# A two-convolution residual block and a spline layer: residual added by DMA, polynomial by Horner, two waits and a table load moved

## The chip, the cores and the metric

The kernel runs on one core of one Trainium2 chip. A core has a matrix engine (PE, its weight loads are listed as PEld), a vector engine (DVE), an activation engine (ACT), GpSimd (POOL), a queue engine (SP) and 16 DMA engines; they run side by side and order themselves by semaphores. The metric is the device time of one execution in microseconds, the median over several runs.

## What is computed

x has the shape (32, 64, 56, 56) in fp32. The first part is a residual block:

```
out = relu(batchnorm(conv3x3(x, sign(w1))))
out = batchnorm(conv3x3(out, sign(w2)))
z   = relu(out + x)
```

The batch norms take mean and variance over the whole batch, so a convolution must be finished before its norm is known. The second part is a spline with clamped position, per element, with a curve for each of the 64 channels:

```
u = (clip(z*a + b, -1.5, 1.5) + 1) * 0.5 * 31;  i = floor(u);  t = clip(u - i, 0, 1)
y = id_gain*z + bias + sum_r mix[c,r] * (alpha[i-1,r]*b0(t) + alpha[i,r]*b1(t) + alpha[i+1,r]*b2(t) + alpha[i+2,r]*b3(t))
```

b0 to b3 are the cubic basis polynomials; the four knot indices are clipped to 0..31.

## The kernel before

Two images lie on the 128 partitions (2 x 64 channels), which makes 16 pairs. The convolutions go through the pairs, each image split in a high and a low fp16 part, and write y1 and y2 to scratch in DRAM. `norm` computes a scale and a bias (BN2_S, BN2_B) on DVE after each of them, with one square root on ACT (line 427).

The spline works on chunks: half a pair, 128 x 1568 elements, 32 chunks in all, two or three in flight. A position is brought to a fixed-point number; its high part is a cell, its low part a signed distance (`offset`) from the nearest of 17 centres. For each chunk and channel five piecewise constant tables are needed: T_NEAR (cube), T_FAR (the cube beyond a distance of 1), T_SQ, T_LIN and T_VAL. PE sums each table in PSUM as steps times 0/1 masks: T_NEAR and T_FAR take four groups of masks ("quads"), the other three take two. PSUM holds two tables at a time, so PE may start a table only when DVE has used the one two places before it (`table`, wait on `table_used`); the order is NEAR, FAR, SQ, LIN, VAL, then NEAR of the next chunk.

What one chunk asks of the others, by the names of the code:

- SP: `load` brings the chunk of y2 to `zbuf` (called `place`) and the chunk of x to `lin` (line 871; it waits until the output that used this `lin` before is stored), `spread` copies the cells to four partition groups in 16 DMAs, `store` writes `lin` out.
- DVE: `total` (line 1016, lin = zbuf * BN2_S + x), `fixed` (1022), `linear` (1028), `near_cube` (1067), `far_cube` (1075), `far_part` (1083), two `middle` masks (1045), `add_table` for T_SQ (1090), `near_part` (1098, times the squared distance), `slope` (1105, T_LIN times offset), `add_slope` (1113), `offsets` (1037), `add_table` for T_VAL (1090) and `finish` (1121, lin = poly * AMP + lin).
- ACT: `far_distance` (961), `position` (930, from `lin` to `zbuf`), `far_square` (968), `cells` (938), `distance_square` (975), `distance` (954), and two `edge` masks (982).
- POOL: `add_far` (919), a DMA that adds the `far` tile onto `lin`, once a chunk.

The work of one loop body belongs to several chunks: in the body of chunk c, DVE finishes c-1 and sums the masks of c+1, and `total`, `position`, `fixed`, `linear`, `cells`, `spread` and `offsets` belong to c+2. The order is the order of the code; each engine has its own. ACT's engine and DVE's wait in place, so what stands behind a waiting instruction waits too.

Between the two parts stands the end of a block: all engines meet there, and SP comes to it only after its waits for the y2 stores.

## Time and profile before

| | us |
|---|---|
| median of 3 runs | 1256.26 (1254.87 to 1257.54) |
| profiled execution, whole | 1254.66 |
| its span, first to last instruction | 1252.8 |
| DVE busy | 1062.8 (85%) |
| PE busy | 1058.6 (85%) |
| ACT busy | 868.8 (69%) |
| POOL busy | 113.4 (9%) |

The busy shares are means over stages that differ: the convolutions fill roughly the first 427 us, the spline the rest. In the spline a busy share near one on an engine says that work in its own order is never late there; a wait printed behind a row ("<-") names what came last before the row could start. A figure "x56" is a count of instructions. An idle wait of an engine that is not the last one costs nothing, so the rows have to be read in pairs: who waits, and what the releaser itself was doing before.

### The profile page before, as it was taken

What the parts mean: (1) busy time and instruction counts of PE and PEld (TensorE: products, weight loads), DVE (VectorE), ACT (ScalarE), POOL (GpSimd) and SP (SyncE); (2) the same over time, 40 slices, a digit from 0 to 9 for tenths busy, and PEclk for the clock granted to TensorE, in tenths of its full rate; (3) what the DMA queues carried; (4) which work ended last, traced back from release to release, by engine and by line L of the source; (5) the groups of instructions that cost most, each with busy time, mean ns of one, the idle gap of its engine ahead of it and who ended that gap; (6) DMA issues with size and microseconds to landing.
All of it is one profiled execution on the core that took longest, in us unless ns stands there. A gap on an engine that the chain in (4) does not pass through costs nothing. (4 is left out here: it accounts for less than half of the span.)

```text
span 1252.8 us, 51454 instructions
## 1 busy us (share of the span) xinstructions
PE 1058.6 (85%) x23562; PEld 710.2 (57%) x23562; DVE 1062.8 (85%) x951; ACT 868.8 (69%) x424; POOL 113.4 (9%) x189
## 2 busy tenths in 40 slices
PE   6999996999999368887888788878887888788876
PEld 4688885788888234554545455444544545455444
DVE  5765656766666689999999999999999999999987
ACT  4454544777787267688868877887788778877881
POOL 6000000282000000000000000000000000000000
PEclk9999998999999778998989889898998989889898
DMA  7666766576777386677767766777677667776552
GB/s 227 259 257 256 276 255 225 217 277 252 271 264 300 136 235 181 183 216 194 185 189 213 196 181 193 208 192 184 189 214 192 184 197 206 194 182 197 157 114 78
DMA packets 58215, 260.85 MB, mean 208 GB/s; under 512 B 16336, under 2 KB 16336, under 8 KB 50000
## 3 DMA queue, kind: packets, MB, share of 16 engines
q1 hardware_dynamic: 52528, 230.88, 56.3%
q0 software_dynamic: 4608, 25.69, 11.0%
q8 instruction: 139, 2.28, 0.8%
q10 hardware_dynamic: 928, 1.90, 0.6%
q14 instruction: 12, 0.10, 0.0%
HBM read 104.29 MB, written 77.07 MB: 145 GB/s over the span
## 5 line engine op out<-in xcount | busy, mean ns | idle before, releaser
L1181 PE MATMUL tab<-edge_mask,diag 128*32 128x392 bf16 x10240 | 501.8, 358 | 132.6 <-DVE poly L1090 130.8
L1181 PEld LDWEIGHTS tab<-edge_mask,diag 128*32 128x32 f16 x10240 | 281.7, 104 | 339.0 <-DVE poly L1090 143.4
L982 ACT ACTIVATE edge_mask<-cell,thr 128x6272 bf16<-128x6272 bf16 x62 | 338.5, 5508 | 0.0
L711 PE MATMUL acc<-split,w 64*64 64x392 f16 x4608 | 195.9, 329 | 12.0 <-DVE w L463 10.8
L711 PE MATMUL acc<-band_split,w 64*64 64x392 f16 x4608 | 197.9, 330 | 9.4 <-ACT band_split L368 7.2
L410 ACT ACTIVATE yout<-acc 128x1568 f32<-128x1568 f32 x64 | 94.2, 1473 | 160.6 <-PE acc L711 139.4
L1181 PE MATMUL tab<-middle_mask,diag 128*32 128x392 bf16 x4096 | 183.4, 332 | 25.0 <-DVE middle_mask L1052 25.0
L711 PEld LDWEIGHTS acc<-band_split,w 64*64 64x64 f16 x4608 | 164.1, 107 | 42.9 <-issue 14.1
L711 PEld LDWEIGHTS acc<-split,w 64*64 64x64 f16 x4608 | 155.3, 107 | 51.9 <-issue 12.6
L520 DVE BATCH_NORM_STATS2 stats<-yout 128x392 f32 (+1 forms) x240 | 118.0, 555 | 60.2 <-ACT yout L410 59.4
L930 ACT ACTIVATE zbuf<-lin,cst 128x1568 f32<-128x1568 f32 x32 | 54.3, 1697 | 163.8 <-DVE lin L1016 157.9
L1181 PEld LDWEIGHTS tab<-middle_mask,diag 128*32 128x32 f16 x4096 | 107.7, 99 | 92.2 <-DVE middle_mask L1052 25.1
L919 POOL DMA_DIRECT2D lin<-far x32 | 50.0, 1564 | 897.5 <-DVE far L1083 897.5
L1090 DVE SCALAR_TENSOR_TENSOR poly<-tab,first,poly 128x1568 f32<-128x1568 f32 x61 | 112.6, 1845 | 0.1
L1045 DVE TENSOR_SCALAR middle_mask<-cell,thr 128x6272 bf16<-128x6272 bf16 x62 | 111.9, 1847 | 0.0
L486 DVE SCALAR_TENSOR_TENSOR band_split<-band_split,xin 128x1568 f16<-128x1568 f16 x30 | 52.5, 1793 | 35.0 <-ACT band_split L389 35.0
L1075 DVE SCALAR_TENSOR_TENSOR far<-tab,first,far 128x1568 f32<-128x1568 f32 x31 | 57.3, 1847 | 8.8 <-PE tab L1181 8.6
L497 DVE SCALAR_TENSOR_TENSOR split<-split,xin 128x3136 f16<-128x3136 f16 (+4 forms) x19 | 55.1, 2913 | 10.7 <-ACT split L400 10.5
L1083 DVE SCALAR_TENSOR_TENSOR far<-far,cst,far_sq 128x1568 f32<-128x1568 f32 x32 | 59.3, 1852 | 2.9
L1016 DVE SCALAR_TENSOR_TENSOR lin<-zbuf,cst,lin 128x1568 f32<-128x1568 f32 x32 | 59.0, 1846 | 3.1 <-PEq L90 3.1
L1121 DVE SCALAR_TENSOR_TENSOR lin<-poly,cst,lin 128x1568 f32<-128x1568 f32 x31 | 57.4, 1852 | 3.3
L1113 DVE SCALAR_TENSOR_TENSOR poly<-far_sq,poly 128x1568 f32<-128x1568 f32 x32 | 57.4, 1793 | 3.1
(126 smaller groups left out, 816.9 us busy)
## 6 DMA issues: line engine op xcount, KB each, us to landing
y_scratch<-yout SPq DMA_DIRECT2D x32, 1568.0 KB, 6.2
cell<-cell SPq DMA_DIRECT2D x496, 98.0 KB, 3.3
xin<-y_scratch SPq DMA_DIRECT2D x16, 1568.0 KB, 9.0
zbuf<-y_scratch SPq DMA_DIRECT2D x32, 784.0 KB, 5.9
lin<-in_x SPq DMA_DIRECT2D x32, 784.0 KB, 6.1
lin<-far POOLq DMA_DIRECT2D x32, 784.0 KB, 8.8
out<-lin SPq DMA_DIRECT2D x31, 784.0 KB, 4.1
xin<-in_x SPq DMA_DIRECT2D x15, 1568.0 KB, 9.3
```

What stands on the lines that cost most here:

```text
L410: act.activation(yout[b][:, :].rearrange("p (r k x) -> p k r x", r=2, k=TILES)[:, 2 * part:2 * part + 2], acc[:, 4 * part:4 * part + 4, 0: ...
L520: dve.bn_stats(stats[:, bass.ds(COUNTS * (g - base) + t, 1), :], yout[b][:, own]).then_inc(counted, 1)
L711: mm = pe.matmul(acc[h * C:(h + 1) * C, 2 * k + r, 0:TILE], weights[part][own, tap * C:(tap + 1) * C], image[own, first:first + ROWS, dx:d ...
L982: act.activation(mask_of(b, q)[:, :, :], cell4[b % 2][:, :, :], ACT.Sign, bias=thr[:, q:q + 1]).then_inc(sign_mask_ready, 1)
L1016: dve.scalar_tensor_tensor(out=lin[b % BUFS][:, :], in0=place[b % 2][:, :], scalar=cc(BN2_S), in1=lin[b % BUFS][:, :], op0=ALU.mult, op1=A ...
L1045: dve.tensor_scalar(mask_of(b, q)[:, :, :], cell4[b % 2][:, :, :], thr[:, q:q + 1], None, ALU.is_ge).then_inc(mask_ready, 1)
L1075: dve.scalar_tensor_tensor(out=quarters(far), in0=summed(i, b, T_FAR), scalar=base(i, b, T_FAR), in1=quarters(far), op0=ALU.add, op1=ALU.m ...
L1083: dve.scalar_tensor_tensor(out=far[:, :], in0=far[:, :], scalar=cc(AMP), in1=far_sq[:, :], op0=ALU.mult, op1=ALU.mult).then_inc(far_part_r ...
L1090: dve.scalar_tensor_tensor(out=quarters(poly[b % 2]), in0=summed(i, b, t), scalar=base(i, b, t), in1=quarters(poly[b % 2]), op0=ALU.add, o ...
L1113: dve.scalar_tensor_tensor(out=poly[b % 2][:, :], in0=far_sq[:, :], scalar=1 / POINT, in1=poly[b % 2][:, :], op0=ALU.mult, op1=ALU.add).th ...
L1121: dve.scalar_tensor_tensor(out=lin[b % BUFS][:, :], in0=poly[b % 2][:, :], scalar=cc(AMP), in1=lin[b % BUFS][:, :], op0=ALU.mult, op1=ALU. ...
L1181: mm = pe.matmul(tab[(b + t) % 2][j * GROUP:(j + 1) * GROUP, sub, 0:SUB], keep["diag"][part][:, j % 2, t, q, :], mask_of(b, q)[:, j, sub * ...
```

## The change

1. x is no longer loaded by SP and added by DVE. ACT writes y * BN2_S into `lin` (`scale`), and POOL issues a DMA that adds the chunk of x from DRAM onto it (`add_x`); `position` then waits for that DMA. It is done for chunks 2 to 31; chunks 0 and 1 keep `total`. ACT scales chunk c+3 in the body of chunk c, and POOL issues `add_x(c+3)` behind `add_far(c)`.
2. The polynomial is evaluated as ((near + sq)*d + lin)*d + val with the signed distance d: `near_part`, `slope` and `add_slope` become `times_offset`, `add_table` and `times_offset`. The squared distance (`distance_square` on ACT) is gone, and with it a tile.
3. On DVE `fixed` stands ahead of `near_cube`, where `total` stood.
4. SP's waits for the last y2 stores move from the end of the convolution block to behind the first spread of the spline block, and `load` stands ahead of `store`.
5. The first ACTIVATE of the kernel is a square root in place of an identity.
6. Two mask tiles change places in memory, and semaphores count by one.

```diff
-        stored = [sem(f"y_stored{b}") for b in range(2)]
+        stored = keep["y_stored"]
...
@@ -283,8 +283,6 @@
             for b in range(2):
                 sp.wait_ge(stored[b], 16 * half_rounds)
             rounds(sp, 1, lambda i, n: body(i, n, y2, 1))
-            for b in range(2):
-                sp.wait_ge(stored[b], 32 * half_rounds)
...
-            act.activation(tmp[:, 5:6], row_scale[:, 0:1], ACT.Identity)
+            act.activation(tmp[:, 5:6], row_scale[:, 0:1], ACT.Sqrt)
...
+        middle_mask = [sb(f"middle_mask{q}", [P, 4, CHUNK], BF16) for q in range(len(MIDDLE_QUADS))]
         edge_mask = [[sb(f"edge_mask{s}{q}", [P, 4, CHUNK], BF16) for q in range(len(EDGE_QUADS))] for s in range(2)]
-        middle_mask = [sb(f"middle_mask{q}", [P, 4, CHUNK], BF16) for q in range(len(MIDDLE_QUADS))]
...
-        dist_sq = sb("dist_sq", [P, CHUNK])
...
@@ -862,13 +860,10 @@
             def load(i, b):
 
                 ysrc = part(y2, i, b)
-                xsrc = part(x, i, b)
-                before, free = in_front(sp, BUFS * i + b - 1), in_front(sp, 16 * (i + b // BUFS))
+                before = in_front(sp, BUFS * i + b - 1)
                 wait_past(sp, offset_ready, before)
                 wait_past(sp, cell_ready, before)
                 sp.dma_start(place[b % 2][:, :], ysrc).then_inc(y_loaded[b % 2], 16)
-                wait_past(sp, stored[b % BUFS], free)
-                sp.dma_start(lin[b % BUFS][:, :], xsrc).then_inc(x_loaded[b % BUFS], 16)
...
             spread(0, 0)
+            for b in range(2):
+                sp.wait_ge(keep["y_stored"][b], 16 * PAIRS)
             load(0, 2)
             spread(0, 1)
 
             def body(i, b, n):
+                if exists(n, b + 3):
+                    load(i, b + 3)
                 if exists(n, b - 1):
                     store(i, b - 1)
-                if exists(n, b + 3):
-                    load(i, b + 3)
                 if exists(n, b + 2):
                     spread(i, b + 2)
...
+            def add_x(c):
+
+                pool.wait_ge(scaled, c - 1)
+                pool.dma_start(lin[c % BUFS][:, :], x[c // 2][:, (c % 2) * CHUNK:(c % 2 + 1) * CHUNK],
+                               accum_op=ALU.add).then_inc(x_added, 16)
+
             def add_far(c):
 
-                pool.wait_ge(far_part_ready, 2 * c + 2)
+                pool.wait_ge(far_part_ready, c + 1)
                 pool.dma_start(lin[c % BUFS][:, :], far[:, :], accum_op=ALU.add).then_inc(far_added, 16)
 
+            add_x(2)
             for c in range(CHUNKS):
                 add_far(c)
+                if c + 3 < CHUNKS:
+                    add_x(c + 3)
...
+            def scale(i, b):
+
+                c = BUFS * i + b
+                act.wait_ge(y_loaded[b % 2], 16 * (2 * i + b // 2 + 1))
+                wait_past(act, stored[b % BUFS], 16 * (i + b // BUFS))
+                act.activation(lin[b % BUFS][:, :], place[b % 2][:, :], ACT.Identity,
+                               scale=cc(BN2_S)).then_inc(scaled, 1)
+
             def position(i, b):
 
                 c = BUFS * i + b
-                act.wait_ge(sum_ready, c + 1)
+                if isinstance(c, int) and c < 2:
+                    act.wait_ge(sum_ready, c + 1)
+                else:
+                    act.wait_ge(x_added, 16 * (c - 1))
                 act.activation(place[b % 2][:, :], lin[b % BUFS][:, :], ACT.Identity, bias=cc(U_B),
                                scale=cc(U_S)).then_inc(place_ready, 1)
...
                 act.wait_ge(far_ready, c + 1)
-                wait_past(act, slope_ready, 2 * c)
+                wait_past(act, far_part_ready, c)
                 act.activation(far_sq[:, :], far[:, :], ACT.Square).then_inc(far_sq_ready, 1)
-
-            def distance_square(i, b):
-
-                c = BUFS * i + b
-                act.wait_ge(offset_ready, c + 1)
-                wait_past(act, near_ready, 2 * c)
-                act.activation(dist_sq[:, :], offset[b % 2][:, :], ACT.Square,
-                               scale=1 / POINT).then_inc(dist_sq_ready, 1)
...
             distance(0, 0)
+            scale(0, 2)
 
             def body(i, b, n):
-                following, after = exists(n, b + 1), exists(n, b + 2)
+                following, after, third = exists(n, b + 1), exists(n, b + 2), exists(n, b + 3)
                 far_distance(i, b)
                 if after:
                     position(i, b + 2)
                 far_square(i, b)
                 if after:
                     cells(i, b + 2)
-                distance_square(i, b)
                 if following:
                     distance(i, b + 1)
-                    edge(i, b + 1, EDGE_QUADS[0])
+                if third:
+                    scale(i, b + 3)
                 if following:
-                    edge(i, b + 1, EDGE_QUADS[1])
+                    for q in EDGE_QUADS:
+                        edge(i, b + 1, q)
 
             rounds(act, body)
...
                 dve.wait_ge(fixed_ready, c + 1)
-                wait_past(dve, dist_sq_ready, c - 1)
-                wait_past(dve, slope_ready, 2 * (c - 2) + 1 if not isinstance(c, int) or c >= 2 else 0)
+                wait_past(dve, slope_ready, c - 1 if not isinstance(c, int) or c >= 2 else 0)
...
-            def near_part(i, b):
-
-                c = BUFS * i + b
-                dve.wait_ge(table_used, used(i, b, T_SQ))
-                dve.wait_ge(dist_sq_ready, c + 1)
-                dve.tensor_tensor(poly[b % 2][:, :], poly[b % 2][:, :], dist_sq[:, :], ALU.mult).then_inc(near_ready, 2)
-
-            def slope(i, b):
-
-                c = BUFS * i + b
-                dve.wait_ge(far_part_ready, 2 * c + 2)
-                dve.wait_ge(table_ready, used(i, b, T_LIN))
-                dve.scalar_tensor_tensor(out=quarters(far_sq), in0=summed(i, b, T_LIN), scalar=base(i, b, T_LIN),
-                                         in1=quarters(offset[b % 2]), op0=ALU.add, op1=ALU.mult).then_inc(table_used, 1)
-
-            def add_slope(i, b):
-
-                c = BUFS * i + b
-                dve.wait_ge(table_used, used(i, b, T_LIN))
-                dve.wait_ge(near_ready, 2 * c + 2)
-                dve.scalar_tensor_tensor(out=poly[b % 2][:, :], in0=far_sq[:, :], scalar=1 / POINT,
-                                         in1=poly[b % 2][:, :], op0=ALU.mult, op1=ALU.add).then_inc(slope_ready, 2)
+            def times_offset(i, b, t, done):
+
+                dve.wait_ge(table_used, used(i, b, t))
+                dve.scalar_tensor_tensor(out=poly[b % 2][:, :], in0=offset[b % 2][:, :], scalar=1 / POINT,
+                                         in1=poly[b % 2][:, :], op0=ALU.mult, op1=ALU.mult).then_inc(done, 1)
...
             def body(i, b, n):
                 previous, following, after = exists(n, b - 1), exists(n, b + 1), exists(n, b + 2)
                 if previous:
-                    add_table(i, b - 1, T_VAL, slope_ready, 2 * (BUFS * i + b - 1) + 2)
+                    add_table(i, b - 1, T_VAL, slope_ready, BUFS * i + b)
                     finish(i, b - 1)
                 if after:
-                    total(i, b + 2)
+                    fixed(i, b + 2)
                 near_cube(i, b)
                 if after:
-                    fixed(i, b + 2)
                     linear(i, b + 2)
                 far_cube(i, b)
                 far_part(i, b)
@@ -1163,9 +1155,9 @@
                     for q in MIDDLE_QUADS:
                         middle(i, b + 1, q)
                 add_table(i, b, T_SQ, table_used, used(i, b, T_NEAR))
-                near_part(i, b)
-                slope(i, b)
-                add_slope(i, b)
+                times_offset(i, b, T_SQ, near_ready)
+                add_table(i, b, T_LIN, near_ready, BUFS * i + b + 1)
+                times_offset(i, b, T_LIN, slope_ready)
                 if after:
                     offsets(i, b + 2)
 
```

DVE, in the opening of the spline, from the last table of chunk 0 to the far cube of chunk 1 (`zbuf` is the position, `lin` the sum, `tab` the table in PSUM), before:

```order
L1090 SCALAR_TENSOR_TENSOR poly<-tab,plain,poly 128x1568
L1121 SCALAR_TENSOR_TENSOR lin<-poly,cst,lin 128x1568
L1016 SCALAR_TENSOR_TENSOR lin<-zbuf,cst,lin 128x1568
L1067 SCALAR_TENSOR_TENSOR poly<-tab,first,poly 128x1568
L1022 TENSOR_SCALAR zbuf<-zbuf,cst 128x1568
L1028 TENSOR_SCALAR lin<-lin,cst,par_sb 128x1568
L1075 SCALAR_TENSOR_TENSOR far<-tab,first,far 128x1568
```

and the same place now:

```order
L1100 SCALAR_TENSOR_TENSOR poly<-tab,plain,poly 128x1568
L1114 SCALAR_TENSOR_TENSOR lin<-poly,cst,lin 128x1568
L1033 TENSOR_SCALAR zbuf<-zbuf,cst 128x1568
L1077 SCALAR_TENSOR_TENSOR poly<-tab,first,poly 128x1568
L1039 TENSOR_SCALAR lin<-lin,cst,par_sb 128x1568
L1085 SCALAR_TENSOR_TENSOR far<-tab,first,far 128x1568
```

The sum is gone, and the clamp to fixed point (`fixed`) has moved ahead of the near cube. The other DVE instructions of a chunk keep their number and place.

ACT, at the start of the spline, from the distance of chunk 0 to the masks of chunk 1 (`edge_mask`), before:

```order
L954 ACTIVATE poly<-offset 128x1568
L961 ACTIVATE far<-poly,cst 128x1568
L930 ACTIVATE zbuf<-lin,cst 128x1568
L968 ACTIVATE far_sq<-far 128x1568
L938 ACTIVATE cell<-zbuf,cst 128x1568
L975 ACTIVATE dist_sq<-offset 128x1568
L954 ACTIVATE poly<-offset 128x1568
L982 ACTIVATE edge_mask<-cell,thr 128x6272 x2
```

and now:

```order
L971 ACTIVATE poly<-offset 128x1568
L937 ACTIVATE lin<-zbuf,cst 128x1568
L978 ACTIVATE far<-poly,cst 128x1568
L947 ACTIVATE zbuf<-lin,cst 128x1568
L985 ACTIVATE far_sq<-far 128x1568
L955 ACTIVATE cell<-zbuf,cst 128x1568
L971 ACTIVATE poly<-offset 128x1568
L937 ACTIVATE lin<-zbuf,cst 128x1568
L991 ACTIVATE edge_mask<-cell,thr 128x6272 x2
```

Line 937 is `scale`; it stands once ahead of the far distance of chunk 0 and then once a body between the distance and the masks. The squared distance is gone.

POOL's queue was 32 times `add_far`. It now begins:

```order
L916 DMA lin<-in_x 128x1568
L922 DMA lin<-far 128x1568
L916 DMA lin<-in_x 128x1568
L922 DMA lin<-far 128x1568
L916 DMA lin<-in_x 128x1568
L922 DMA lin<-far 128x1568
```

Line 916 is `add_x`, of chunks 2, 3 and 4 here; line 922 is `add_far`, of chunks 0, 1 and 2.

## Rows read from the trace of the kernel before

**Rows 1.** Windows, the spline stage: busy time and count of each engine, granted clock, DMA

```profile
427.00:1253.00 826.00, 663.28 (x14336) 389.41 (x14336) 789.02 (x488) 621.23 (x254) 50.04 (x32) 0.90 0.69 185
```

**Rows 2.** Waits, 484 to 1200 us: total us, times, longest

```profile
PE tab L1181 <- DVE poly L1090: 122.5, 29, 4.4
...
DVE far L1075 <- PE tab L1181: 1.9, 7, 0.4
```

**Rows 3.** Timeline of DVE, one chunk: start us, us, instruction

```profile
859.48 1.84 DVE L1075 SCALAR_TENSOR_TENSOR far<-tab,first,far 128x1568 f32<-128x1568 f32 x1
861.42 1.85 DVE L1083 SCALAR_TENSOR_TENSOR far<-far,cst,far_sq 128x1568 f32<-128x1568 f32 x1
...
866.71 1.84 DVE L1090 SCALAR_TENSOR_TENSOR poly<-tab,first,poly 128x1568 f32<-128x1568 f32 x1
...
872.30 1.79 DVE L1113 SCALAR_TENSOR_TENSOR poly<-far_sq,poly 128x1568 f32<-128x1568 f32 x1
...
878.76 1.84 DVE L1016 SCALAR_TENSOR_TENSOR lin<-zbuf,cst,lin 128x1568 f32<-128x1568 f32 x1
880.52 1.84 DVE L1067 SCALAR_TENSOR_TENSOR poly<-tab,first,poly 128x1568 f32<-128x1568 f32 x1
...
884.73 1.85 DVE L1075 SCALAR_TENSOR_TENSOR far<-tab,first,far 128x1568 f32<-128x1568 f32 x1 [0.26 <-PE tab L1181]
```

**Rows 4.** Timeline of PE, two chunks, and windows over one's first table

```profile
618.58 4.19 PE L1181 MATMUL tab<-edge_mask,diag 128*32 128x392 bf16 x64 [4.39 <-DVE poly L1090]
...
868.61 5.42 PE L1181 MATMUL tab<-edge_mask,diag 128*32 128x392 bf16 x64 [4.39 <-DVE poly L1090]
...
881.85 8.13 PE L1181 MATMUL tab<-edge_mask,diag 128*32 128x392 bf16 x192
...
868.60:873.80 5.20, 5.19 (x64) 2.52 (x68) 5.06 (x3) 5.20 (x1) 0.00 (x0) 0.50 0.85 176
```

**Rows 5.** Timelines of DVE and PE, the last two chunks, which have no total

```profile
1216.74 1.85 DVE L1090 SCALAR_TENSOR_TENSOR poly<-tab,first,poly 128x1568 f32<-128x1568 f32 x1
...
1233.89 1.85 DVE L1075 SCALAR_TENSOR_TENSOR far<-tab,first,far 128x1568 f32<-128x1568 f32 x1 [3.46 <-PE tab L1181]
...
1218.64 4.52 PE L1181 MATMUL tab<-edge_mask,diag 128*32 128x392 bf16 x64 [3.95 <-DVE poly L1090]
```

**Rows 6.** Groups of ACT, 484 to 1185 us: busy us, mean ns, idle before

```profile
L930 ACT ACTIVATE zbuf<-lin,cst 128x1568 f32<-128x1568 f32 x28 | 47.5, 1698 | 144.2 <-DVE lin L1016 144.2
...
L975 ACT ACTIVATE dist_sq<-offset 128x1568 f32<-128x1568 int32 x28 | 41.9, 1497 | 0.0
```

**Rows 7.** DMA: line 919 (add_far), queue q0 500 to 1200, load of x

```profile
DMA to landing us min/median/max: 5.9/8.8/12.1
...
q0 software_dynamic: 4032, 22.48, 17.3%
...
lin<-in_x SPq DMA_DIRECT2D x32, 784.0 KB, 6.1
```

**Rows 8.** Timelines at the ends of both convolutions, and the last y2 store

```profile
211.31 1.28 ACT L427 ACT_TABLE_LOAD   x1
...
212.89 0.16 DVE L650 RECIPROCAL tmp<-tmp 128x1 f32<-128x1 f32 x1 [0.98 <-ACT tmp L427]
...
421.36 0.35 SPq L274 DMA_DIRECT2D y_scratch<-yout  x1
...
422.22 0.16 DVE L650 RECIPROCAL tmp<-tmp 128x1 f32<-128x1 f32 x1 [0.25 <-ACT tmp L427]
...
427.49 1.85 DVE L1016 SCALAR_TENSOR_TENSOR lin<-zbuf,cst,lin 128x1568 f32<-128x1568 f32 x1 [3.08 <-PEq L90]
...
y_scratch<-yout SPq DMA_DIRECT2D x1, 1568.0 KB, 5.1
```

**Rows 9.** Timeline of ACT and DVE at the spline's start

```profile
452.90 1.60 ACT L961 ACTIVATE far<-poly,cst 128x1568 f32<-128x1568 f32 x1
...
459.44 1.85 DVE L1075 SCALAR_TENSOR_TENSOR far<-tab,plain,far 128x1568 f32<-128x1568 f32 x1 [1.04 <-PE tab L1181]
```

More of the change, by code:

```diff
@@ L798, in spline @@
         stored = [sem(f"out_stored{b}") for b in range(BUFS)]
+        x_added = sem("x_added")
         far_added = sem("far_part_added")
+        scaled = sem("scaled")
         sum_ready = sem("sum_ready")
@@ L808, in spline @@
         far_sq_ready = sem("far_sq_ready")
-        dist_sq_ready = sem("dist_sq_ready")
         mask_ready = sem("mask_ready")
@@ L1083, in far_part @@
                 dve.scalar_tensor_tensor(out=far[:, :], in0=far[:, :], scalar=cc(AMP), in1=far_sq[:, :],
-                                         op0=ALU.mult, op1=ALU.mult).then_inc(far_part_ready, 2)
+                                         op0=ALU.mult, op1=ALU.mult).then_inc(far_part_ready, 1)
             def add_table(i, b, t, made, count):
@@ L1126, in closing_quarters @@
                 last, b = CHUNKS // BUFS - 1, BUFS - 1
-                dve.wait_ge(slope_ready, 2 * CHUNKS)
+                dve.wait_ge(slope_ready, CHUNKS)
                 dve.wait_ge(far_added, 16 * CHUNKS)
@@ L1243, in build @@
             "lin": [sb(f"lin{b}", [P, CHUNK]) for b in range(BUFS)],
+            "y_stored": [sem(f"y_stored{b}") for b in range(2)],
             "y_loaded": [sem(f"y_loaded{b}") for b in range(2)],
```

## Prediction, written before the changed kernel ran

> **What bounds the kernel now.** I first read the windows by stage. In the spline DVE is busy 789 of 826 us, ACT 621 and PE 663, at a mean granted clock of 0.90 [rows 1]. That makes DVE look like the only bound, and an instruction taken from it like pure gain. The waits say less: DVE waits for PE only 1.9 us in all, before `far_cube`, but PE waits for DVE 29 times, 122.5 us [rows 2], or 4.2 us a chunk, always before the same table, T_VAL, whose place in PSUM `add_table` of T_SQ frees. So I read one chunk in order, from that release.
>
> On DVE the release ends at 866.71 + 1.84 = 868.55 (call it s), and the next `far_cube` starts at 884.73, s + 16.2; from that start to the next release are 866.71 - 859.48 + 1.84 = 9.07 us [rows 3]. A chunk is the sum, 25.25 us there, and 24.98 on average: the `far_cube` of chunk 0 starts at 459.44 and that of chunk 31 at 1233.89, 31 intervals [rows 5, 9]. DVE waited 0.26 us in this chunk, so of the 16.2 us it fills 15.9 itself.
>
> On PE, s releases T_VAL, then come T_NEAR and T_FAR of the next chunk without a gap. T_VAL took 5.42 us here and 4.19 in another chunk; the window over it shows a granted clock of 0.50, the lower level of 1.2 GHz, after an idle time of 4.39 us [rows 4]. The clock is back at 2.4 GHz for the rest: 192 matmuls take 8.13 us, 2.66 for 64 (starts overlap the listed ends by 0.15), so the 256 matmuls of NEAR and FAR take 10.6. FAR is complete at s + 0.06 + 5.2 + 10.6 + 0.2 = s + 16.1, which is where `far_cube` started. With the T_VAL of 4.19 (4.0 start to start) it is s + 14.9. So the two engines are within 1 us of each other over this stretch, and only the other 9.07 us are DVE's alone.
>
> The last chunks are the experiment that the kernel itself makes: no `total`, `fixed`, `linear` or `offsets` stand between. The release ends at 1216.74 + 1.85 = 1218.59, `far_cube` starts at 1233.89, s + 15.3, after 3.46 us of waiting for PE, whose T_VAL took 4.52 at the low clock [rows 5]. Some 4.7 us of DVE work taken away (`total` 1.76, `fixed` and `linear` 3.95 - 1.85 = 2.1 [rows 3], `offsets` about 0.9) moved `far_cube` from about s + 15.9 by 0.6. That is the row on which my forecast rests.
>
> **The change, part by part.** The sum is made against the profiled execution, 1254.66 us whole; the median of the runs is 1256.26, 1.6 above it, and I add that at the end.
>
> Square root first: the first batch norm waits 0.98 us for ACT, behind a table load of 1.28, the second 0.25 with no load [rows 8]. The load goes, and the identities, relus and signs run after a square root in both programs: -0.7. The Trainium skill, ScalarE: Activation LUTs, What ACT_TABLE_LOAD costs, puts a switch at 2.66 us with its drain; by it the term would be up to -2.7, but the trace's load is hidden in part, and the 1.28 row agrees with the page's 1283 ns for the load proper.
>
> The y2 wait: the last store is issued at 421.36 and takes 5.1 us, so it lands at 426.5; DVE had been idle 3.08 us when it began at 427.49, 1.0 after the landing [rows 8]. Without the wait the blocks meet when DVE is done, at 424.4, and the same 1.0 follows: -2.1. Behind the moved wait on SP stands the load of chunk 2, which is not issued until the first spread is out, long after; nothing pays for it. Bounds: 0 to -3.
>
> Spline's start: this is new waiting. Before, the far distance of chunk 0 starts on ACT at 452.9 and the first `far_cube` at 459.44 [rows 9]. Now `scale` of chunk 2 (not shown by this trace; 1.5 to 1.7 by the two ACT passes [rows 6]) comes ahead, then POOL issues `add_x`, which must land before `position`, and DVE's `fixed` stands ahead of its first near cube. Chain, in the old times: 452.9 + 1.6 + 0.3 to the issue, landing 5.9 at least and 8.8 at the median of the only such DMA [rows 7], `position` 1.7, then `fixed`, near cube and `linear`, 884.73 - 0.26 - 880.52 = 3.95 [rows 3]: `far_cube` at 466.4 to 469.3 in place of 459.44. The DMA is nearly alone there, so I take a landing of 6.5 and a loss of +7.5 (bounds +7 to +10; a load of x by SP takes 6.1).
>
> Each chunk, DVE: `total` goes, 1.76 start to start [rows 3]; three polynomial passes stay three, all fp32 at 1.79 to 1.85; but each now waits for the one before it, one more such dependence of about 0.15. `fixed` only changes place. DVE could be at `far_cube` at s + 15.9 - 1.6 = s + 14.3, and its own period would be 23.4.
>
> Each chunk, PE: NEAR still cannot start before `add_table` of T_LIN has ended, s + 3.9. If the clock does not fall, FAR is there at s + 3.9 + 10.6 + 0.2 = s + 14.7, a period of 23.8. If it falls as now, s + 14.9 to 16.1 [rows 4], s + 15.3 in [rows 5]: periods of 24.0 to 25.2. What PE idles before T_VAL shrinks only from 4.2 to about 3.7, because that idle time lies in the 9.07 us that stay (9.07 less SQ and LIN, 5.3); at 3.95 the clock still fell [rows 5]. So it falls in most chunks, with a slow stretch that has a little less idle time in it. I take 24.3 on average, near the last chunks' 15.3 + 9.07 = 24.4. That is 0.7 less than 24.98; it counts in the 29 intervals in which a `total` stood: -19.7 (bounds 23.8 and 25.0: -34 to 0).
>
> Each chunk, DMA: `far_part` ends, POOL issues `add_far` 0.3 later and `add_x(c+3)` 1.6 behind it on the same queue. From 500 to 1200 us the 28 `add_far` took 17.3% of the 16 engines' 700 us, 4.3 us each [rows 7], so x needs about 4 to 5.5 us behind the landing of `add_far` at 8.8: 12.8 to 14.3 after the first issue (call it X). Behind X stand `position` 1.75, 3.95 for `fixed`, near cube and `linear`, then `far_cube` to the end of `far_part`, 861.42 + 1.85 - 859.48 = 3.8: the loop closes in X + 9.8. Up to X = 14.5 it fits in 24.3. I charge +3 for the few landings near the 12.1 maximum, which would each stretch a chunk by about 2. ACT exchanges a pass of 1.5 for one of 1.6; it waits 144.2 us in 28 chunks [rows 6], 5.1 each, which covers that and the wait for the stored output that `scale` inherits from SP's load. SP loses a DMA a chunk, and the y2 load no longer stands behind a store. Nothing for these, with up to +3 if the cover fails in places. The Trainium skill, DMA: Bandwidth & Descriptors, Anatomy of one DMA, fits such a DMA as 2.0 us plus bytes over 436 GB/s, an estimate of 3.8 us for 803 KB. No row agrees with it here, the shortest accumulation is 5.9 and the median 8.8; by the page X would be under 9 and the queue no subject at all.
>
> Sum: 1254.66 - 0.7 - 2.1 + 7.5 - 19.7 + 3 = 1242.7, and with the 1.6 to the median 1244.3. I predict 1244.
>
> **The rivals.**
>
> A. The DVE count is all that matters: 1.6 a chunk. For it speaks DVE's share in [rows 1]; against it the 3.46 us of waiting as soon as work goes [rows 5]. 1256.3 - 2.8 + 7.5 - 29 x 1.6 = 1215.
>
> B. The clock holds because PE idles less: period 23.8, -34. 1256.3 - 2.8 + 7.5 - 34 = 1227. Against it speaks that it fell after 3.95.
>
> C. Slower: POOL's queue becomes the loop. It decides from X = 15.2, where X + 9.8 is the old 24.98. Were the two accumulations to land one full latency after the other, X would be 17.6, the period 27.4 and the time 1256 + 29 x 2.4 + 5 = 1331; an X of 16 gives 25.8 and 1285. For it: one DMA already reached 12.1, x comes from DRAM and not from the core's own memory, and masks are being spread at the same moment. Against: the data of `add_far` keep the engines busy only about 4 of its 8.8 us, so the second one's fixed part lies beside the first.
>
> D. PE gives nothing back: the low clock covers T_VAL wholly in every chunk (s + 16.1), or the queue takes the 0.7 (X about 15). Then only start and block end are left, 1256.3 - 2.8 + 7.5 = 1261 at the worst, 1254 to 1261 in all.
>
> **How the numbers follow.** Forecast (periods of 24.0 to 24.6, 1234 to 1253): 0.66. A: 0.04. B: 0.10. C: 0.10. D: 0.10. The range is 1228 to 1260: it leaves out A, half of B's low side and nearly all of C. A change within 0.2%, 2.5 us, cannot be told from none here. Faster takes the forecast, A, B, which is 0.80; same, 1253.7 to 1258.8, most of D, 0.08; slower C and the rest of D, 0.12.
>
> **What would show it.** After: `far_cube` waiting for PE about 1 us in most chunks, T_VAL still in 4 to 5.4 us behind an idle time of about 3.7, and the starts of `far_cube` 24.3 apart. DVE's first `far_cube` near 464.5. No table load at 211, no 3 us of idle time before the spline's first DVE instruction. Landings of the x accumulation 11 to 13 us after their issue, and ACT's `position` waiting for them little. If `position` waits for `add_x` in every chunk and `fixed` waits for `position`, C holds. If the far cube does not wait for PE at all, A. If the clock shows full in the T_VAL windows, B. The weakest number is X, because no row has two accumulations back to back.

## The result, and the profile after

The changed kernel takes 1269.05 us, the median of 4 runs (1268.45 to 1271.71); the kernel before took 1256.38 in the same comparison. The ratio is 1.0108 [1.0093, 1.0123]: 1.1% slower, where 1244 us had been forecast, outside the range of 1228 to 1260. Two of the twelve executions of kernel 1 below fell in a slow state (1440.2 and 2160.7 us); they are in its median of 1256.04 and not in its ratio.

The forecast had named what to look at. The starts of the kernel came out as forecast. Timelines of DVE in the changed kernel (start us, us, instruction, in brackets the idle time ahead and what ended it), at the first batch norm, at the spline's first instruction and at its first far cube:

```profile
211.93 0.16 DVE L648 RECIPROCAL tmp<-tmp 128x1 f32<-128x1 f32 x1 [0.26 <-ACT tmp L425]
...
425.54 1.85 DVE L1027 SCALAR_TENSOR_TENSOR lin<-zbuf,cst,lin 128x1568 f32<-128x1568 f32 x1 [0.98 <-PEq L90]
...
461.42 1.09 DVE L1033 TENSOR_SCALAR zbuf<-zbuf,cst 128x1568 int32<-128x1568 f32 x1 [11.74 <-ACT zbuf L947]
...
465.20 1.84 DVE L1085 SCALAR_TENSOR_TENSOR far<-tab,plain,far 128x1568 f32<-128x1568 f32 x1
```

The wait of 0.98 behind the table load is 0.26, the 3.08 ahead of the spline is 0.98 [rows 8], and the first far cube starts at 465.20 (464.5 had been forecast; the terms of the sum, 459.44 + 7.5 - 2.8, give 464.1; 459.44 before [rows 9]). What came after it did not. The waits of the steady stretch, 500 to 1200 us (total us, times, longest):

```profile
ACT zbuf L947 <- DMA lin<-in_x: 125.1, 28, 6.1
...
PE tab L1173 <- DVE poly L1100: 109.4, 27, 4.3
...
DVE zbuf L1033 <- ACT zbuf L947: 55.3, 28, 3.3
...
DVE far L1085 <- PE tab L1173: 3.5, 6, 0.9
```

The first and third rows are the mark that the forecast had set for its rival C: in every chunk `position` waits for `add_x` and `fixed` waits for `position`. DVE's far cube hardly waits for PE. The source view of the two accumulations gives their landings (line 916, `add_x`, then line 922, `add_far`):

```profile
DMA to landing us min/median/max: 8.2/14.1/15.4
...
DMA to landing us min/median/max: 5.8/9.4/10.5
```

`add_x` is issued 1.6 us behind `add_far`, so X is 1.6 + 14.1 = 15.7 where 12.8 to 14.3 had been assumed. The chain of waits, followed back through one chunk (start us, us, what the time belongs to), shows that nothing else is in the loop:

```profile
864.94 1.70 ACT zbuf L947
...
866.67 0.05 DVE zbuf L1033
...
867.68 0.43 DVE poly L1077
...
869.45 0.55 DVE lin L1039
...
870.45 1.86 DVE far L1085
...
872.33 1.86 DVE far L1093
...
874.48 1.58 POOL lin L922
876.05 13.99 DMA lin<-in_x
```

From the issue at 874.48 the landing at 890.04 is 15.6 away; before the issue lie 9.54 us, from the start of `position` on. The whole is 25.1, and the far cubes of chunks 1 to 29 are 25.35 apart on average (25.03 before). The loop has no slack, so each late landing is paid in full. Of the whole kernel's chain the page gives to this one DMA:

```profile
DMA lin<-in_x 21%; PE tab L1173 17%; DVE far L1085 4%; DVE middle_mask L1055 4%; DVE far L1093 3%; ACT zbuf L947 3%; POOL lin L922 2%; DVE poly L1100 2%; DVE poly L1077 1%; DVE lin L1039 1%; ACTq L963 1%; DVE poly L1106 0%; ACT cell L955 0%; DVE zbuf L1033 0%; DVE lin L1129 0%
```

DVE is busy 1012.6 us now and was busy 1062.8 before: 50 us of work left the engine with the largest share, and the kernel became slower.

### The profile page after: what moved, and what is told of

It is laid out like the page before. It is cut to its first block, busy times and chain, and to the rows that moved or that the text cites. A ratio compares the mean times of both kernels' runs of the same rounds, so it can differ in the third digit from the quotient of the medians.

```text
span 1267.8 us, 51281 instructions
## 1 busy us (share of the span) xinstructions
PE 1068.0 (84%) x23562; PEld 726.9 (57%) x23562; DVE 1012.6 (80%) x921; ACT 871.0 (69%) x421; POOL 165.0 (13%) x219
## 4 chain that ended last, share of the span: by engine, by line
DMA 21%; PE 17%; DVE 16%; issue 6%; ACT 3%; POOL 2%; ACTq 1%; DVEq 0%
DMA lin<-in_x 21%; PE tab L1173 17%; DVE far L1085 4%; DVE middle_mask L1055 4%; DVE far L1093 3%; ACT zbuf L947 3%; POOL lin L922 2%; DVE poly L1100 2%; DVE poly L1077 1%; DVE lin L1039 1%; ACTq L963 1%; DVE poly L1106 0%; ACT cell L955 0%; DVE zbuf L1033 0%; DVE lin L1129 0%
## 5 line engine op out<-in xcount | busy, mean ns | idle before, releaser
L1173 PE MATMUL tab<-edge_mask,diag 128*32 128x392 bf16 x10240 | 508.3, 358 | 141.6 <-DVE poly L1100 124.2
L1173 PEld LDWEIGHTS tab<-edge_mask,diag 128*32 128x32 f16 x10240 | 292.1, 104 | 343.4 <-DVE poly L1100 136.8
L709 PEld LDWEIGHTS acc<-band_split,w 64*64 64x64 f16 x4608 | 167.6, 107 | 39.7 <-issue 13.1
L1100 DVE SCALAR_TENSOR_TENSOR poly<-tab,first,poly 128x1568 f32<-128x1568 f32 x92 | 169.9, 1847 | 3.3
L1173 PEld LDWEIGHTS tab<-middle_mask,diag 128*32 128x32 f16 x4096 | 110.4, 99 | 90.3 <-DVE middle_mask L1062 22.9
L1106 DVE SCALAR_TENSOR_TENSOR poly<-offset,poly 128x1568 f32<-128x1568 int32 x64 | 114.7, 1792 | 2.2
L1033 DVE TENSOR_SCALAR zbuf<-zbuf,cst 128x1568 int32<-128x1568 f32 x32 | 35.1, 1096 | 76.5 <-ACT zbuf L947 76.5
L916 POOL DMA_DIRECT2D lin<-in_x x30 | 52.4, 1747 | 159.9 <-ACT lin L937 159.9
L978 ACT ACTIVATE far<-poly,cst 128x1568 f32<-128x1568 f32 x32 | 51.3, 1602 | 27.1 <-DMA lin<-far 27.1
## 6 DMA issues: line engine op xcount, KB each, us to landing
lin<-in_x POOLq DMA_DIRECT2D x30, 784.0 KB, 14.1
```

The costliest lines, as they stand in the source:

```text
L709: mm = pe.matmul(acc[h * C:(h + 1) * C, 2 * k + r, 0:TILE], weights[part][own, tap * C:(tap + 1) * C], image[own, first:first + ROWS, dx:d ...
L1100: dve.scalar_tensor_tensor(out=quarters(poly[b % 2]), in0=summed(i, b, t), scalar=base(i, b, t), in1=quarters(poly[b % 2]), op0=ALU.add, o ...
L1106: dve.scalar_tensor_tensor(out=poly[b % 2][:, :], in0=offset[b % 2][:, :], scalar=1 / POINT, in1=poly[b % 2][:, :], op0=ALU.mult, op1=ALU. ...
L1173: mm = pe.matmul(tab[(b + t) % 2][j * GROUP:(j + 1) * GROUP, sub, 0:SUB], keep["diag"][part][:, j % 2, t, q, :], mask_of(b, q)[:, j, sub * ...
```

## The experiments

Each kernel is timed against the kernel before, on the same chip. "Period" is the mean distance of the far cubes of chunks 1 to 29; "first" is where the first far cube starts. Both are read from the one profiled execution, while "us" is the median of all.

| kernel | us | ratio to before | first | period |
|---|---|---|---|---|
| before | 1256.4 | 1 | 459.4 | 25.03 |
| after | 1269.05 | 1.0108 [1.0093, 1.0123] | 465.2 | 25.35 |
| 1 fixed behind near cube | 1256.04 | 1.0009 [0.9994, 1.0024] | 461.1 | 24.96 |
| 2 x ahead of far | 1233.51 | 0.9826 [0.9809, 0.9843] | 465.1 | 24.31 |
| 3 no far accumulation | 1228.67 | 0.9781 [0.9766, 0.9796] | 465.2 | 24.01 |
| 4 before, waits and square root | 1252.40 | 0.9974 [0.9964, 0.9984] | 457.4 | 25.03 |
| 5 both 1 and 2 | 1247.89 | 0.9944 [0.9929, 0.9959] | 461.4 | 24.61 |
| 6 all but the x part | 1252.23 | 0.9973 [0.9964, 0.9983] | 456.0 | 25.03 |
| 7 x part adds a tile | 1243.05 | 0.9897 [0.9880, 0.9914] | 463.5 | 24.51 |
| 8 half of x | 1237.80 | 0.9863 [0.9848, 0.9877] | 462.7 | 24.29 |
| 9 2, and a shorter start | 1226.47 | 0.9769 [0.9756, 0.9782] | 457.6 | 24.26 |
| 10 SP and tiles as before | 1261.68 | 1.0049 [1.0031, 1.0067] | 466.3 | 25.11 |
| 11 before, x part alone | 1267.96 | 1.0092 [1.0076, 1.0107] | 470.5 | 25.13 |
| 12 9, with store ahead of load | 1266.20 | 1.0080 [1.0061, 1.0100] | 457.2 | 25.64 |

**1. Take the near cube out of the loop.**

```diff
-                if after:
-                    fixed(i, b + 2)
                 near_cube(i, b)
                 if after:
+                    fixed(i, b + 2)
                     linear(i, b + 2)
```

> The changed kernel with one edit: fixed stands behind near_cube on DVE again. Theory L (a loop through POOL's queue sets the period: far_part, add_far, add_x behind it, position, fixed, near_cube, linear, far_cube, far_part, X + 9.8 with X = 1.6 + 14.1 = 15.7, 25.5 us a chunk): near_cube, 1.8 us, leaves the loop, which then closes in 23.7, so the far table on PE is last again at about 24.3; 29 x 1.0 less and 1.8 less at the start, about 1239 us. Rival R (16 DMA engines are too full and everything behind them is late alike, or the Horner passes cost it): the wait only moves to another instruction, 1267 to 1270.

It gave back 13 us, the whole loss, but not the 30 that were expected. The waits from 500 to 1200 us:

```profile
ACT zbuf L947 <- DMA lin<-in_x: 113.6, 27, 6.1
...
DVE far L1085 <- PE tab L1172: 30.8, 23, 2.9
PE tab L1172 <- issue: 16.3, 16, 2.1
```

`position` is as late as ever for x, and now PE's share appears: the far cube waits for it 30.8 us, and PE itself loses 16.3 us in 16 places that the profile calls issue. The cells, and ACT's edge masks of the next chunk, stand behind `position` on ACT, and in the timeline all 16 stops fall in tables made of edge masks. That the late masks cause them is a reading and was not tried by itself. Without the near cube the loop should close in X + 8.0 = 23.6, so what sets the 24.96 of this kernel is not shown; 16.3 us of stops in 28 chunks, 0.6 each, would lift PE's 24.3 to about that. What is shown is that taking the near cube from behind the wait gives back the whole loss, 4.1 us of it before the first far cube, although `position` waits for x almost as before.

**2. Issue the x accumulation first.**

```diff
             for c in range(CHUNKS):
-                add_far(c)
                 if c + 3 < CHUNKS:
                     add_x(c + 3)
+                add_far(c)
```

> The changed kernel with one edit: POOL issues add_x(c+3) ahead of add_far(c). Theory L: x is issued when ACT has scaled, about 1.7 us before far_part ends, and no longer waits behind 4 us of far's data; position then waits for far_distance, that is for add_far, which now lands 12 to 13 us after its issue. The loop closes in 0.3 + 12.5 + 1.6 + 1.75 + 3.95 + 3.8 = 23.9, so about 24.3 a chunk and 1242 to 1248 us. Rival R (the amount of accumulation, not its order): the same bytes, the same period, 1267 to 1270.

Swapping two lines moved the kernel from 1269 to 1233.5, better than expected. The source views, `add_x` and then `add_far`:

```profile
DMA to landing us min/median/max: 7.4/8.2/9.1
...
DMA to landing us min/median/max: 5.9/11.2/13.5
```

The 14.1 of x is 8.2, and `add_far` has taken over the queueing, 11.2 for 9.4. `far_distance` waits for that landing, and `position` stands right behind `far_distance` on ACT. So from the issue of `add_far` to the start of `position` the loop now takes 11.2 and 1.5 for `far_distance`, where X was 15.7: about 3 us less. The bytes are the same as in the changed kernel, so the amount of accumulation alone does not make the loss. In the timelines of POOL, ACT, DVE and PE, and in the window over T_VAL, the new order is seen at work:

```profile
869.87 1.68 ACT L947 ACTIVATE zbuf<-lin,cst 128x1568 f32<-128x1568 f32 x1
...
877.14 1.85 DVE L1085 SCALAR_TENSOR_TENSOR far<-tab,first,far 128x1568 f32<-128x1568 f32 x1 [0.65 <-PE tab L1173]
...
878.67 0.86 POOL L916 DMA_DIRECT2D lin<-in_x  x1 [19.80 <-ACT lin L937]
881.18 1.59 POOL L922 DMA_DIRECT2D lin<-far  x1 [1.65 <-DVE far L1093]
...
886.22 4.14 PE L1173 MATMUL tab<-edge_mask,diag 128*32 128x392 bf16 x64 [3.83 <-DVE poly L1100]
...
886.22:890.20 3.98, 3.98 (x65) 2.17 (x68) 3.82 (x3) 2.98 (x1) 0.00 (x0) 0.66 1.00 221
```

`scale` releases `add_x` 2.5 us ahead of `add_far` (at the median x is issued 1.9 us after the start of the far cube, where it was 5.6 in the changed kernel); `position` has no wait of its own; and the far cube waits 0.65 us for PE (28.6 us in 26 chunks of 500 to 1200 us), whose T_VAL still takes 4.14 us, at a mean granted clock of 0.66, behind an idle time of 3.83. That is the picture that had been forecast for the changed kernel (about 1 us of waiting, 3.7 idle). The period, 24.31, is the forecast's too, but this profiled execution took 1238.8 us and was the slowest of five; the 5.3 us down to the median put the period there nearer 24.1.

**3. Leave the other accumulation out.** `add_far` isn't issued, so the far part is missing from the result, and its waiters wait for `far_part`.

```diff
             for c in range(CHUNKS):
-                add_far(c)
                 if c + 3 < CHUNKS:
                     add_x(c + 3)
```

> The changed kernel without the DMA add_far: the far part is computed and never added, and what waited for its landing waits for far_part. Theory L: add_x is alone in its queue, lands 8 to 9 us after its issue, well before position; the period is the one that the prediction put on PE and DVE, 24.3 (23.8 to 24.6), so 1236 to 1244 us. Rival D (PE gives nothing back, the low clock covers the gain): 24.8 or more, 1255 or more. Rival A (DVE alone): 23.4, about 1215.

The period fell to 24.01. The x accumulation lands in 9.1 us at the median:

```profile
DMA to landing us min/median/max: 7.3/9.1/10.2
```

Against 2 the rest of POOL's queue is worth 0.3 us a chunk by the profiled executions, 0.2 by the medians. The far cube waits for PE in all 29 chunks of the stretch, 27.6 us, so PE is last at a period of 24.0. Its clock is low in T_VAL here too: the one at 883.55 takes 4.14 us at a mean of 0.66. The forecast of B (23.8 with a full clock) is nearly the same number for another reason.

**4 and 6. The parts without x.** In 4 the kernel before gets the square root and the moved wait; in 6 the changed kernel gets back `total`, SP's load of x and the order of `store` and `load`, and so keeps Horner, the wait and the square root.

```diff
-                sp.wait_ge(stored[b], 32 * half_rounds)
+                sp.wait_ge(keep["y_stored"][b], 16 * PAIRS)
...
-            act.activation(tmp[:, 5:6], row_scale[:, 0:1], ACT.Identity)
+            act.activation(tmp[:, 5:6], row_scale[:, 0:1], ACT.Sqrt)
```

> The kernel before with two parts of the change only: the first ACTIVATE is a square root, and SP's waits for the y2 stores stand behind the first spread of the spline. All theories: 0.7 + 2.1 less, 1253.5 us; no table load at 211 us, DVE's first spline instruction about 1 us after its last one of the block before.

```diff
                 if after:
-                    fixed(i, b + 2)
+                    total(i, b + 2)
                 near_cube(i, b)
                 if after:
+                    fixed(i, b + 2)
                     linear(i, b + 2)
```

> The change without its first part: x is loaded by SP and summed by DVE as before, the Horner form, the moved y2 wait and the early square root stay. Theory L: the Horner passes wait each for the one before, 0.15 a chunk more on DVE, which is the bound here again: 1252.4 + 4, 1255 to 1257 us. Rival H (the Horner form is what made the change slow): 1262 or more.

Both come to 1252.3: 3.3 us gained by the ratio, for the two waits (2.8 had been forecast), and nothing from Horner, neither way; the 4 us that had been expected in 6 for its longer chain of waits did not come. Their period is the 25.03 of before.

**5. Both orders at once.** The edits of 1 and 2 together.

```diff
+                near_cube(i, b)
                 if after:
                     fixed(i, b + 2)
-                near_cube(i, b)
-                if after:
                     linear(i, b + 2)
```

> The changed kernel with both edits: add_x ahead of add_far on POOL, and fixed behind near_cube on DVE. Theory L: with x first the loop through POOL is already shorter than what PE and DVE need (24.3 a chunk), so taking near_cube out of it gives nothing more per chunk; the first near cube no longer waits for x, 1.9 less at the start: 1230 to 1235 us against the 1233.5 of x first alone. Rival S (fixed is what ACT's cells wait for, and the masks behind them are late on PE): slower than x first alone, 1238 or more.

Wrong by 13 us: it is slower than 2 alone. The waits of 500 to 1200 us:

```profile
ACT far L978 <- DMA lin<-far: 100.3, 29, 4.5
...
DVE lin L1114 <- DMA lin<-far: 27.3, 23, 2.5
ACT lin L937 <- DMA out<-lin: 26.0, 15, 3.1
```

and the timeline of POOL and of DVE around one pair of issues:

```profile
858.54 1.60 POOL L916 DMA_DIRECT2D lin<-in_x  x1 [20.18 <-ACT lin L937]
860.13 1.77 POOL L922 DMA_DIRECT2D lin<-far  x1
...
873.53 1.85 DVE L1114 SCALAR_TENSOR_TENSOR lin<-poly,cst,lin 128x1568 f32<-128x1568 f32 x1 [1.52 <-DMA lin<-far]
```

`near_cube` ahead of `fixed` brings the cells, and with them `scale`, about 2 us later with respect to the far cube. `scale` now ends when `far_part` does (858.24 and 858.25), the head start of x is gone, and `add_far` is issued behind it, 1.9 us after the end of `far_part` where 0.3 would do. DVE's `finish` waits for it. That the queue is the loop again, entered at its other end, is one reading. The other is the rival that stood in the expectation, late masks: PE has 9 stops called issue here, 6.4 us, all in tables made of edge masks, and none in 2. Over the whole stretch `finish` waits for `add_far` 27.3 us (1.6 in 2), and `scale` waits for the stored output 26.0 us (11.7 in 2), so the cells are not all that delays it. The run does not tell these shares apart; the period is 0.3 us longer than in 2, 8 us in 28 chunks.

**7 and 8. What makes x late.** In 7 `add_x` adds a tile of zeros from the core's memory, of the same size, so the residual is left out for these chunks; in 8 it adds only half of the columns of x.

```diff
-                pool.dma_start(lin[c % BUFS][:, :], x[c // 2][:, (c % 2) * CHUNK:(c % 2 + 1) * CHUNK],
+                pool.dma_start(lin[c % BUFS][:, :], still[:, :],
```

> The changed kernel with one edit: add_x reads a tile of zeros in the core's own memory in place of x in DRAM, so the residual is left out. Theory L with the source as its cause: the second accumulation lands about 4 us behind the first, X = 14.3 in place of 15.7, a period of 24.3 and 1242 to 1250 us. If the place in the queue alone decides: it lands 6 us behind as before, and the time stays at 1265 to 1270.

```diff
-                pool.dma_start(lin[c % BUFS][:, :], x[c // 2][:, (c % 2) * CHUNK:(c % 2 + 1) * CHUNK],
+                pool.dma_start(lin[c % BUFS][:, 0:CHUNK // 2], x[c // 2][:, (c % 2) * CHUNK:(c % 2) * CHUNK + CHUNK // 2],
```

> The changed kernel with one edit: add_x moves only the first 784 of the 1568 columns, so half of the residual is left out. Theory L: half of x's data leaves the queue, about 2.3 us; X = 13.4, the loop closes in 23.2 and the far table on PE is last, 24.0 to 24.4 a chunk, 1236 to 1243 us. Rival F (a fixed latency per DMA, not its data, is what position waits for): landing at 13 us or more, 1260 or more.

Landings of `add_x` in 7 and in 8:

```profile
DMA to landing us min/median/max: 7.2/12.4/14.1
...
DMA to landing us min/median/max: 5.7/11.1/13.2
```

X is 14.0 with a tile as the source, 12.7 with half the bytes, 15.7 in the changed kernel. Both dropped under the point where the loop decides, and both kernels fell near PE's floor. A source in DRAM is 1.7 us of the 15.7, and the second half of the bytes 3.0. Most of the 1.7 is not in x's own part: `add_far` itself lands after 8.1 in 7, where it took 9.4.

**10 and 11. The rest of the change put back, and x alone.** 10 is the changed kernel with SP's `store` ahead of `load` and the mask tiles in their old places; 11 is the kernel before with the x part only.

```diff
-                if exists(n, b + 3):
-                    load(i, b + 3)
                 if exists(n, b - 1):
                     store(i, b - 1)
+                if exists(n, b + 3):
+                    load(i, b + 3)
```

> The changed kernel with SP's order (store ahead of load) and the place of the two mask tiles as before. Both theories put no time on these: 1267 to 1270 us, X within 0.3 us of 15.7. If they matter, the time moves by more than 3 us.

> The kernel before with the first part of the change alone (x accumulated by DMA, total gone from chunk 2 on, fixed ahead of near_cube); the old polynomial, the old waits and the table load stay. Theory L: the loop through POOL's queue does not contain the polynomial behind far_part, so the period is 25.4 as in the whole change, and the start costs the same: 1269 + 2.8 = 1270 to 1274 us. If the Horner form had a share in the slowing, this one is faster than the whole change.

The x part alone costs 11.6 us by the ratio, so it is the main cause; the whole change costs 13.6 by the same measure. 10 came 7 us under the changed kernel where at most 3 were expected. So the x part costs 11.6, the two waits give 3.3, and `load` ahead of `store` or the places of the mask tiles cost another 7; that these add up to 15 and not 13.6 is within the intervals. Its waits and the landing of `add_x`:

```profile
ACT zbuf L947 <- DMA lin<-in_x: 99.6, 27, 6.1
...
ACT lin L937 <- DMA zbuf<-y_scratch: 41.3, 24, 5.5
...
DMA to landing us min/median/max: 8.1/13.7/15.1
```

The load of y2 is issued 3.4 us later with respect to the far cube, after x has landed, and `scale` has to wait for it; in this order of POOL's queue that costs nothing, since `add_x` stands behind `add_far`. The landing of x is 0.4 shorter at the median. Taken one by one over chunks 1 to 28, X is 15.64 on average in the changed kernel, 15.37 in 10 and 15.29 in 11, which also has the old order and places, with a period of 25.13. 28 times the 0.27 is 7.6 us, so a shorter X accounts for the size. Why X is shorter stays open: that the earlier load of y2 in the changed kernel slows x by sharing the engines would fit, but the two edits of 10 were not tried apart.

**9 and 12. The best version, and a warning.** 9 is 2, and besides chunk 2 is summed by `total` as chunks 0 and 1 are, with its `fixed` behind the near cube of chunk 0, so that the opening is as before. 12 is 9 with SP's `store` ahead of `load`.

```diff
+                if isinstance(i, int) and i == 0 and b == 2:
+                    sp.dma_start(lin[b][:, :], part(x, i, b)).then_inc(x_loaded[b], 16)
...
+                opening = isinstance(i, int) and i == 0 and b == 0
+                if opening:
+                    total(i, b + 2)
```

> The changed kernel with add_x ahead of add_far, and with chunk 2 handled as chunks 0 and 1: SP loads its x, DVE sums it in the body of chunk 0, fixed(2) stands behind near_cube(0) there. Theory L: the steady part is that of x first alone (24.3 a chunk), and the spline's start loses its 11.7 us wait for position: the first far cube at 457.5 in place of 465.1, so 1225 to 1229 us against 1233.5. Rival: the first chunks have slack elsewhere and the 7.5 us come back in the next bodies, 1231 or more.

> The kernel of e9_start with SP's store ahead of its load again. The output's store then does not share the engines with the load of y2, so scale waits less for it (11.7 us over 27 chunks with x first) and x is issued a little earlier: 0 to 3 us less than e9_start. If far's landing or the far table on PE is last anyway: the same.

9 took 7 us from 2, as expected: the first far cube is at 457.6 in place of 465.1. It beats the kernel before by 2.3% and the changed one by 3.4%. 12, for which 0 to 3 us less were expected, is 40 us slower than 9. Timelines of SP, ACT, POOL and DVE in 12, one chunk:

```profile
861.20 1.85 DVE L1114 SCALAR_TENSOR_TENSOR lin<-poly,cst,lin 128x1568 f32<-128x1568 f32 x1 [3.25 <-DMA lin<-far]
...
863.08 0.35 SPq L888 DMA_DIRECT2D out<-lin  x1
863.74 1.22 SPq L866 DMA_DIRECT2D zbuf<-y_scratch  x1
...
870.86 1.60 ACT L938 ACTIVATE lin<-zbuf,cst 128x1568 f32<-128x1568 f32 x1 [2.17 <-DMA zbuf<-y_scratch]
...
872.75 1.06 POOL L918 DMA_DIRECT2D lin<-in_x  x1 [23.12 <-ACT lin L938]
873.81 1.77 POOL L924 DMA_DIRECT2D lin<-far  x1
...
887.16 1.85 DVE L1114 SCALAR_TENSOR_TENSOR lin<-poly,cst,lin 128x1568 f32<-128x1568 f32 x1 [1.46 <-DMA lin<-far]
```

This is a closed ring: `finish` (861.20) releases `store`, the load of y2 stands behind it (863.74) and is there at 870.8, `scale`, `add_x`, and behind that `add_far` (873.81), whose landing releases the next `finish` at 887.16, 25.96 later. In this chunk every member waits for the one before it; from 500 to 1200 us `scale` waits for the load of y2 27 times and `finish` for `add_far` 21 times. Harmless in 10, the order of `store` and `load` on SP closes the ring as soon as x stands first on POOL's queue.

## Why the prediction was wrong, step by step

- Square root and y2 wait (-2.8): held. The rows show 0.7 and 2.1, kernel 4 gained 3.3 us.
- Spline's start (+7.5): held in its first figure. The first far cube came 0.7 later than the 464.5 of the forecast and 1.1 later than the 464.1 that its own terms give; against kernel 4, which has the two waits, it is 7.8 later. The x accumulation alone on its queue landed in 8.2 where 6.5 had been taken. That the start was worth this much is shown by 9 against 2: 7 us.
- Horner: held at nothing (6 against 4: 0.2 us); the 0.15 a chunk charged to DVE for it does not show in the time.
- Each chunk, PE and DVE at 24.3 and not at DVE's 23.4 nor at the old 24.98: held, but only where the queue lets it show, as in 2 (24.31) and 8 (24.29). The fit of 2 to the second digit is luck, since its median execution lies lower. Rival A is out: with the same DVE work taken away no kernel's period came below 24.0, where A had 23.4, and in 3 the far cube waits for PE in every chunk. Rival B is out: T_VAL stays slow behind 3.83 us of idle time. Rival D's first reason, that PE gives nothing back, is out by the same two kernels; its second, the queue, went further than D had it.
- Each chunk, DMA: this is the step that failed: "x needs about 4 to 5.5 us behind the landing of `add_far` at 8.8: 12.8 to 14.3 after the first issue". Measured: by the medians `add_far` lands after 9.4 and x 6.3 behind it, 15.7. The loop rule "X + 9.8" itself was right where the loop is the one it describes. With the averages of X it gives 25.4 for the changed kernel (15.64), 25.2 for 10 (15.37) and 25.1 for 11 (15.29); measured are 25.35, 25.11 and 25.13. With X of 14.0 and 12.7 it gives less than PE's 24.0 to 24.3, and the measured periods are 24.51 and 24.29. In 1 and 5, where `fixed` stands behind the near cube, the queue and the masks on PE are not told apart, and no such sum was shown to hold.
- SP's order and the mask tiles at nothing: failed too, by 7 us (10 against the changed kernel). The prediction counted the load of y2 ahead of the store as free.

So the likeliest case and rival C changed places over 1.4 us of an accumulation's landing. In the sum, the -19.7 and the +3 became 28 x 0.32 = +9, which with the +5.8 up to the first far cube (the waits' -2.8 already in it) makes +15 between the profiled spans (1252.8 and 1267.8); between the medians it is +12.7. That "the second one's fixed part lies beside the first" stood in no row. The engines' time of an accumulation is 4.5 us here, near the 4.3 of the prediction, but the landings are 6 apart. What I had in hand and did not use: the maximum of 12.1 for a single `add_far` and the fact that the loop has no slack. In a loop without slack a median landing above 14.5 is not a tail to be charged with +3; it is the period. The queue's term had deserved its full range, 12.8 to 17.6, in the forecast and not only in a rival.

The chance of 0.12 for slower was too small for a second reason. The order of two lines on POOL was taken as given. In the changed kernel `scale` ends 2.0 us after the start of the far cube, and `far_part` 3.7 us after it, so x was ready first and the queue stood idle for it. ACT asks for `add_far` (`far_distance`) directly ahead of x (`position`), so it needs both landings; by the medians the second of them comes 19.7 us after the start of the far cube in the changed kernel and 15.3 in kernel 2, and nothing but the order of these two lines decides between 1269 and 1233.5.

## What to carry to other kernels

Where two DMAs share a queue, list for each when its data are ready and when its waiter wants it, and compare the orders by the last landing that an engine needs. Here the one that was ready first had to go first, although its waiter stands second on its engine. Then check that it is still released first in the kernel as it runs, since a queue is served in its own order: in 5 and 12 x came too late and held `add_far` back. Work taken from the busiest engine counts only up to the next loop: write every loop down as a sum that closes on itself, and treat a term of it that no row shows as the forecast's main risk. A move that is free in one order of a queue can cost 40 us in another, so orders are tried together, not one by one.

## What the runs showed of the hardware

An accumulating DMA on POOL's queue holds the DMA engines far longer than a plain one with the same bytes on SP's. The DMA view of the changed kernel, 500 to 1200 us (queue, packets, MB, share of 16 engines):

```profile
q1 hardware_dynamic: 29099, 88.46, 47.6%
q0 software_dynamic: 7975, 44.40, 35.3%
```

and of the kernel before the row of the plain DMAs, whose other row is in [rows 7]:

```profile
q1 hardware_dynamic: 33284, 110.79, 54.0%
```

The plain queue lost 6.4% of 700 us with the 28 loads of x, about 1.6 us each; q0 gained 18.0% (35.3 less 17.3) with 28 accumulations, 4.5 us each, for the same 803 KB. The two queues differ in kind as well (software and hardware), and no kernel here issues a plain DMA of this size from POOL, so how much of the 4.5 is the accumulation itself is not shown. Two on one queue land 6.1 us apart at the median, pair by pair, although they are issued 1.6 apart. From the core's own memory instead of DRAM the gap is 6.0, so the source hardly matters to it; with half the bytes it is 3.3. Alone on the queue, in the spline's opening, the accumulation from DRAM landed in 7.0 us (kernels 1, 5 and 11) to 8.4 (2), and in 8.2 in the changed kernel; in the steady part of 3, also without a second one, in 9.1 at the median. The shortest one from the core's memory took 5.8. The Trainium skill, DMA: Bandwidth & Descriptors, Anatomy of one DMA, gives an estimate of 3.8 us for a DMA of this size; no accumulation of the full size came under 5.8 us here, alone or queued.
